# A four-layer graph network on one core: each distance product gets a bank of its own, and the transposed state, the messages and the distances become one block on TensorE

## The chip, the cores and the metric

The kernel runs on one core of a Trainium2 chip. The core has five engines with a queue each: TensorE (PE in the profile, with PEld for its weight loads), VectorE (DVE), ScalarE (ACT), GpSimd (POOL) and SyncE (SP), which only issues transfers here. They take their own instructions in order and wait for one another by semaphores. TensorE writes its products into PSUM, which has eight banks of 128 partitions by 512 fp32 values; this kernel uses all eight. The metric is the device time in microseconds (us) of one execution; lower is better.

## What is computed

Sixteen graphs of 512 nodes with 128 features go through four layers, each with a residual and a layer norm. Cut to what matters, for one graph:

```
# layer 0: gated message passing
h     = conv17(relu(bn(conv1(x))));  x_conv = relu(bn(h) + x)
s     = x @ w_se.T + b_se
A     = exp(-|s_i - s_j|^2)                      # distance products, then exp
msg   = relu(x @ w_msg.T + b_msg)                # messages
x_nmp = (A * adj) @ msg
r, z  = sigmoid(gates of [x_conv, x_nmp], x);  n = tanh(gi_n + r * gh_n)
x1    = layernorm(x + (1 - z) * n + z * x)       # "state" Y, transposed, then normed
# layer 1: attention
X, q, k = leaky(x1 @ W_lin + b), leaky(x1 @ W_q), leaky(x1 @ W_k)
A     = adj * sigmoid(q k^T / sqrt(128)); attended = D^-1/2 A D^-1/2 X
x2    = layernorm(x1 + attended)                 # residual Z1
# layer 2: tangent space
support = adj @ (artanh(|x2|)/|x2| * x2);  x3 = layernorm(x2 + project(expmap0(support)))
# layer 3: degree-normed aggregation, linear, relu
out   = layernorm(x3 + relu(D^-1/2 (adj + I) D^-1/2 x3 W + b))
```

## The kernel before

The graphs go through a software pipeline written out by hand. In **slot** t the front stage (layer 0) of graph t, the middle stage (layer 1) of graph t-1 and the rear stage (layers 2 and 3) of graph t-2 run side by side. Slots 0 to 3 are written out, slots 4 to 14 are a loop, and `ending` writes out slot 15 and the drain of the last two graphs. On each engine a function `body` lists the pieces of a slot in a fixed order; every piece waits for semaphores named after what is ready. The counts `n["f"]`, `n["m"]`, `n["r"]` (and `f_prev`, `m_prev`, `r_prev`) are the graphs that a stage has finished when the piece of this slot (or of the last one) is done. The chunks c = 0 to 3 are blocks of 128 nodes.

The eight banks are CONV (convolution), F0 and F1 (messages, keys, gates), C0 and C1 (distances, attention logits, gates), K0, K1, K2 (many short uses). The profile leaves numbers out of names, so K0, K1 and K2 are all `K` there.

The seam of the slot is where the gates of graph t-1 end and its state goes on to layer 1, while the front stage of graph t begins. Before the change it runs as follows.

- DVE at the end of a slot: `reset`, `rest_of_h1`, `new_input` (L1054, needs the last gate product), `stacked` (L721 and L723, the two factors STL and STR of the distances, from K0 and from ACT's ZR at L433), `kept_state` (L770, XT from the update gate WG), `gated` (L762, L765: the state Y).
- ACT: the update gate WG (L532), ZL and ZR, the tanh (L448), a load of the activation table (L539), four exps of the distances (L453), the copy `keep_x` (L472), four degree sums (L486), the copy X1T of the transposed normed state (L480), the relu of the messages, the copies of queries and keys, the second norm X2 (L414), a logarithm, another table load (L553), the copy XRAW of the linear rows (L506), and four sigmoids of the attention logits (L458).
- PE: distances 0 and 1 into C0 and C1 (L1297), the four transposes of Y into K0 (`state_by_nodes`, L1319), distances 2 and 3 into C0 and C1 again after the exps of 0 and 1, the messages into F0 (L1225), eight taps of the convolution, the four transposes of X1 (L1219), some taps, query, key and linear rows (`projections`; L1351, L1353, L1225), taps, the attention logits (L1364; product c+2 goes into the bank of c after its sigmoid), the support of layer 2 (L1232), the taps of the sum (into K0), and so on. The last aggregation of the rear stage is at L1400.
- DVE at the head of a slot: statistics of the transposed state (`first_norm_stats`, L668), the residual Z1 of layer 1 with its four statistics in between (`first_residual`, L991 and L996), the normed state X1 (`first_norm`, L692), the moments of the second norm, `message_sum` (L829), the sum of H1, the small terms of artanh, `leaky` (L835, L838), `leaky_linear` (L843, needs XRAW), `degree_guard` and `tangent` (the factor and FX at L817, which the support needs), `attention01` (L751: sigmoid times adjacency), `masked0` (L824), `attention23`, `own_loops`, `conv_part` (L944, needs the taps of the sum), `ball_factor`, `second_residual` and its moments, `scaled_norm` (FS at L926, needed by L1400).
- POOL raises variances to the power -0.5 (L336).

Of the kernel before, what the change touches and what calls it, by code (L numbers as in the profile page):

```python
# [68 lines left out]
def adj_resnorm_kernel(nc, xT_d, adjT_d, adj_d, mask_d, weights_d, less_d, rows_d, params_d, sqmat_d, ident_d, out_d):  # L69
    ctx = ExitStack()  # L70
    with ctx:
# [86 lines left out]

        CONV, F0, F1, C0, C1, K0, K1, K2 = (bank(n) for n in ("CONV", "F0", "F1", "C0", "C1", "K0", "K1", "K2"))
        CB = (C0, C1)  # L160

        ev = {n: sem("s_" + n) for n in EVENTS + LN_EVENTS + DMA_EVENTS}
        s_const, s_leading, s_split, s_prep = (sem(n) for n in ("s_const", "s_leading", "s_split", "s_prep"))
# [237 lines left out]
        def _(act):  # L401
# [48 lines left out]
            def exps(n, a, b):  # L450
                for c in range(a, b):
                    act.wait_ge(ev["dist_done"], nth(c, n["f"]))
                    A(A0[:, c, :], CB[c % 2][:, :], ACT.Exp).then_inc(ev["exp_ready"], 1)  # L453

            def sigmoids(n, a, b):
                for c in range(a, b):
# [176 lines left out]
        def _(dve):  # L633
# [150 lines left out]

            def first_norm_stats(n):
                dve.wait_ge(ev["yt_done"], n["m"])
                norm_stats(0, lambda c: cols(K0, c), n["m"])

            def artanh_series(n):
                V.reciprocal(T[:, 8, :], T[:, 2, :])  # L790
# [35 lines left out]

            def message_sum(n):
                dve.wait_ge(ev["msg_done"], n["f"])
                V.tensor_tensor(MSG[:, :, :], chunked(F0), ROWS[:, :].unsqueeze(1).to_broadcast([P, C, P]),  # L829
                                ALU.add).then_inc(ev["msg_sum"], 1)  # L830

            def leaky(n):
# [153 lines left out]
            def first_residual(n, count, previous):  # L986
                dve.wait_ge(ev["x2_ready"], every(previous))

                def residual(c):
                    dve.wait_ge(ev["agg1_done"], nth(finished(n, c), count))  # L990
                    V.scalar_tensor_tensor(Z1[:, c, :], cols(attended_bank(n, c), c), DINV[:, c:c + 1], first_norm_of(n)[:, c, :],  # L991
                                           ALU.mult, ALU.add).then_inc(ev["z1_ready"], 1)

                def stats(c):
                    dve.wait_ge(ev["z1_ready"], nth(c, count))
                    return V.bn_stats(ST[:, 1, c, :], Z1[:, c, :])  # L996

                residual(0)
                residual(1)
                stats(0)  # L1000
                residual(2)
                stats(1)
                residual(3)
                stats(2)
                stats(3).then_inc(ev["ln1_stats"], 1)

            def second_norm_moments(count):
                norm_moments(1, count)
# [1 line left out]
                                       ALU.add).then_inc(ev["var_ready"], 1)  # L1010

            def first_norm(n):
                norm_apply(0, lambda c: cols(K0, c), first_norm_of(n), n["m"], ev["x1_ready"])

            def output(n):
                dve.wait_ge(ev["out_stored"], 16 * (B - 1))
# [39 lines left out]
            def body(t, mid, rear):  # L1056
# [6 lines left out]
                if mid:  # L1063
                    first_norm(n)
                if rear:
                    second_norm_moments(n["r"])
                message_sum(n)
                if not n["first"]:
# [4 lines left out]
                    artanh_series(n)  # L1073
                if mid:
                    leaky(n)
                    leaky_linear(n)
                if rear:
                    degree_guard(n)
                    tangent(n)
                if mid:  # L1080
                    attention01(n)
                masked0(n)
# [22 lines left out]
                reset(n)  # L1105
                if following:
                    rest_of_h1(n["f_next"], n["f"])
                new_input(n)
                if following:
                    stacked(n["f_next"])  # L1110
                    kept_state(n["f"])
                    gated(n["f"])

            def ending():
                a, b, c = counts(dve, B - 1), counts(dve, B), counts(dve, B + 1)
                first_norm_stats(a)
                first_residual(a, a["r"], a["r_prev"])
                first_norm(a)
                second_norm_moments(a["r"])
                message_sum(a)  # L1120
                sum_of_h1(a["f"], a["f_prev"])
# [1 line left out]
                artanh_ratio(a)  # L1123
                artanh_series(a)
                leaky(a)
                leaky_linear(a)
                degree_guard(a)
                tangent(a)
                attention01(a)
                masked0(a)  # L1130
                attention23(a)
# [17 lines left out]
                first_norm_stats(b)  # L1149
                first_norm(b)  # L1150
                first_residual(a, a["m"], a["m_prev"])
                second_norm_moments(a["m"])
                leaky(b)
                leaky_linear(b)
# [9 lines left out]
                scaled_attention(b)  # L1164
                ball_factor(b)
                first_residual(b, b["m"], b["m_prev"])
                second_norm_moments(b["m"])
                second_residual(b)
                tangent_norm(c)
# [22 lines left out]
        def _(pe):  # L1192
# [85 lines left out]
            def sum_taps(n):  # L1278

                pe.wait_ge(ev["hsl_ready"], n["f"])  # L1280
                pe.wait_ge(ev["str_ready"], n["f"])
                pe.wait_ge(ev["x_raw"], n["m"])
                if n["first"]:
                    pe.wait_ge(s_split, 4)
                taps(S_SUM, 0, ODD, K0[:, 0:PH], HSH[:, :], HSL[:, :], ODD).then_inc(ev["conv2_sum"], 1)
# [7 lines left out]
                                  stop=(last and k == 3 * len(terms)))  # L1293
                return done

            def distances(c):
                mm(CB[c % 2][:, :], cols(STL, c), STR[:, :], start=True, stop=True).then_inc(  # L1297
                    ev["dist_done"], 1)

            def first_taps(n):  # L1300
                pe.wait_ge(ev["h1_ready"], n["f"])
# [2 lines left out]
                    pe.wait_ge(s_split, 2)  # L1304
                even_taps(0, 8)

            def distances01(n):
                pe.wait_ge(ev["str_ready"], n["f"])
                pe.wait_ge(ev["w_ready"], n["f_prev"])
                distances(0)  # L1310
                pe.wait_ge(ev["gate_u"], n["f_prev"])
                distances(1)

            def state_by_nodes(n):
                pe.wait_ge(ev["y_ready"], n["m"])
                pe.wait_ge(ev["d_kept"], n["m_prev"])
                pe.wait_ge(ev["str_ready"], n["f"])
                for c in range(C):
                    last = nc.tensor.transpose(cols(K0, c), cols(Y, c), IDENT[:, :])  # L1319
                last.then_inc(ev["yt_done"], 1)  # L1320

            def distances23(n):
                pe.wait_ge(ev["exp_ready"], nth(0, n["f"]))
                distances(2)
                pe.wait_ge(ev["exp_ready"], nth(1, n["f"]))
                distances(3)

            def messages(n):
                pe.wait_ge(ev["gate_t"], n["f_prev"])
                pe.wait_ge(ev["x_loaded"], 16 * n["f"])  # L1330
                if n["first"]:
                    pe.wait_ge(s_plain_w, 48)
                    pe.wait_ge(s_less, 1)
                rows_of(F0, X_IN, plain(F_MSG)).then_inc(ev["msg_done"], 1)

            def first_norm_by_features(n):
                if not n["drain"]:
# [3 lines left out]
            def support(n):  # L1341
                pe.wait_ge(ev["xt_ready"], n["r"])
                if not n["drain"]:
                    pe.wait_ge(ev["adjr_loaded"], 16 * n["r"])
                if not n["last"]:
                    pe.wait_ge(ev["res_scaled"], n["r_prev"])
                aggregate_nodes(lambda c: support_bank(n, c), adjacency(n), FX, ev["agg2_done"])

            def projections(n):
                pe.wait_ge(ev["x1t_ready"], n["m"])  # L1350
                mm(query_bank(n)[:, :], plain(F_Q), X1T[:, :], start=True, stop=True).then_inc(ev["q_done"], 1)  # L1351
                pe.wait_ge(ev["msg_sum"], n["f"])
                mm(F0[:, :], plain(F_K), X1T[:, :], start=True, stop=True).then_inc(ev["k_done"], 1)  # L1353
                rows_of(K0, X1T, plain(F_LIN)).then_inc(ev["x_done"], 1)

            def attention(n):
                pe.wait_ge(ev["q_ready"], n["m"])
                pe.wait_ge(ev["k_ready"], n["m"])
                for c in range(C):
                    if c < 2:  # L1360
                        pe.wait_ge(ev["exp_ready"], nth(c + 2, n["f"]))
# [118 lines left out]

            def ending():
                a, b, c = counts(pe, B - 1), counts(pe, B), counts(pe, B + 1)
                distances01(a)
                state_by_nodes(a)
                distances23(a)
                messages(a)
                first_taps(a)
                first_norm_by_features(a)
                even_taps(8, EVEN)
# [99 lines left out]
```

## Time and profile before

| | |
|---|---|
| median of 3 runs | 797.41 us (796.39 to 798.12) |
| the profiled execution | 798.0 us, its span 796.2 us |
| mean granted clock of TensorE | 0.964 of full speed |
| busy, PE / DVE / ACT / POOL | 715.7 (90%) / 625.2 (79%) / 424.7 (53%) / 135.3 us (17%) |
| one slot of the loop | 45.3 us (from one `new_input` to the next) |

The span runs from the first to the last instruction of the profiled execution. A busy share is a mean over the whole span; a matmul counts as busy while it is in the pipeline, so a PE that is busy nine tenths of the time can still have waits that matter. The time of an engine's wait stands in brackets behind the instruction that ended it, with the instruction that released it.

### The profile page before, as it was taken

The page shows a single profiled execution, that of the slowest core. Times are in us where ns is not written, and L with a number is a line of the kernel's source. Part 1 is how long each engine was busy: PE and PEld are TensorE (multiplying, and loading weights), DVE is VectorE, ACT ScalarE, POOL GpSimd, SP SyncE. Part 2 cuts the span into 40 slices and gives each one's busy share as a digit, 9 for nine tenths or more (in the row PEclk, how much of TensorE's full clock was granted, in tenths as well). Part 3 has the DMA queues.
Part 4 walks back from the last instruction along what each step waited for, and adds up shares of the span by engine and source line. Part 5 has one row for each costly group of instructions (what it writes and reads, how often), then busy time and mean ns, then how long its engine had stood idle before and what let it go on. Part 6 is the DMA issues. An engine that isn't in the chain of part 4 may idle for free.

```text
span 796.2 us, 12758 instructions
## 1 busy us (share of the span) xinstructions
PE 715.7 (90%) x3984; PEld 542.6 (68%) x3984; DVE 625.2 (79%) x2080; ACT 424.7 (53%) x881; POOL 135.3 (17%) x151
## 2 busy tenths in 40 slices
PE   3889999999999999999999999999999999998653
PEld 1766777777676877767776777767677776765531
DVE  7456788888878887888888888887888888876655
ACT  4164737556473755657373755647374655624431
POOL 0000111211122111211121121121121121111221
PEclk8889999999999999999999999999999999999776
DMA  5303241150605133060514224060423215101000
GB/s 198 119 14 129 97 158 68 57 169 14 224 14 171 66 108 116 23 215 13 193 44 162 75 66 158 13 224 13 171 66 122 102 45 192 54 14 54 0 14 27
DMA packets 46586, 75.33 MB, mean 95 GB/s; under 512 B 4065, under 2 KB 12769, under 8 KB 46433
## 3 DMA queue, kind: packets, MB, share of 16 engines
q1 hardware_dynamic: 46560, 75.02, 27.6%
q8 instruction: 12, 0.20, 0.1%
q14 instruction: 14, 0.11, 0.0%
HBM read 70.82 MB, written 4.19 MB: 94 GB/s over the span
## 4 chain that ended last, share of the span: by engine, by line
DVE 40%; PE 36%; issue 11%; ACT 9%; POOL 3%; DVEq 1%; DMA 0%; SPq 0%; ACTq 0%; POOLq 0%
PE K L1400 7%; DVE BIG L751 5%; PE C L1292 4%; PE CONV L1266 4%; DVE A L824 4%; PE F L1292 3%; ACT X L414 2%; DVE X L692 2%; POOL RSTD L336 2%; DVE Z L866 2%; ACT L553 2%; PE F L1353 2%; DVE FS L926 2%; DVE Z L991 2%; DVE ST L668 2%
## 5 line engine op out<-in xcount | busy, mean ns | idle before, releaser
L336 POOL TENSOR_TENSOR RSTD<-VEPS,POW 128x4 f32<-128x4 f32 x48 | 48.8, 1017 | 341.6 <-DVE VEPS L686 341.6
L1266 PE MATMUL CONV<-H1H,WH 128*128 128x256 f32 x288 | 85.6, 297 | 0.0
L1266 PE MATMUL CONV<-H1L,WH 128*128 128x256 f32 x288 | 81.4, 283 | 0.0
L1266 PE MATMUL CONV<-H1H,WL 128*128 128x256 f32 x288 | 81.2, 282 | 0.0
L1400 PE MATMUL K<-ADJR,FS 128*128 128x512 f32 x112 | 52.9, 617 | 10.1 <-DVE FS L926 10.1
L1364 PE MATMUL C<-QT,KT 128*128 128x512 f32 x128 | 61.6, 606 | 0.1
L1232 PEld LDWEIGHTS K<-XS,BIG 128*128 128x128 f32 x496 | 57.8, 192 | 1.3
L1232 PE MATMUL K<-XS,BIG 128*128 128x128 f32 x496 | 57.9, 275 | 0.0
L1232 PEld LDWEIGHTS K<-FX,ADJR 128*128 128x128 f32 x448 | 51.1, 192 | 9.9 <-issue 8.2
L1372 PE MATMUL F<-A,MSG 128*128 128x512 f32 x128 | 57.5, 592 | 0.0
L1266 PEld LDWEIGHTS CONV<-H1L,WH 128*128 128x128 f32 x288 | 55.2, 192 | 0.0
L1266 PEld LDWEIGHTS CONV<-H1H,WH 128*128 128x128 f32 x288 | 55.2, 192 | 0.0
L1266 PEld LDWEIGHTS CONV<-H1H,WL 128*128 128x128 f32 x288 | 55.1, 191 | 0.0
L1232 PE MATMUL K<-FX,ADJR 128*128 128x128 f32 x448 | 53.4, 277 | 0.0
L523 ACT ACTIVATE XCH<-XC,BI 128x512 fp32r<-128x512 f32 x16 | 11.5, 722 | 68.2 <-DVE XC L950 68.2
L453 ACT ACTIVATE A<-C 128x512 f32<-128x512 f32 x64 | 34.8, 595 | 23.1 <-PE C L1297 23.1
L458 ACT ACTIVATE BIG<-C 128x512 f32<-128x512 f32 x64 | 38.0, 596 | 15.4 <-PE C L1364 14.1
L1400 PEld LDWEIGHTS K<-ADJR,FS 128*128 128x128 f32 x112 | 20.8, 196 | 36.4 <-issue 36.4
L500 ACT ACTIVATE JUNK<-K 128x128 bf16<-128x128 f32 x60 | 15.8, 277 | 50.4 <-PE K L1232 50.4
L1364 PEld LDWEIGHTS C<-QT,KT 128*128 128x128 f32 x128 | 21.6, 188 | 28.6 <-ACT BIG L458 19.5
L751 DVE TENSOR_TENSOR BIG<-BIG,ADJM 128x512 f32<-128x512 f32 x60 | 39.9, 685 | 1.4 <-ACT BIG L458 1.4
L824 DVE TENSOR_TENSOR A<-A,ADJF 128x512 f32<-128x512 f32 x64 | 39.8, 685 | 0.0
(251 smaller groups left out, 1932.1 us busy)
## 6 DMA issues: line engine op xcount, KB each, us to landing
ADJF<-in_adjT SPq DMA_DIRECT2D x16, 1024.0 KB, 5.3
ADJN<-in_adj SPq DMA_DIRECT2D x16, 1024.0 KB, 7.7
ADJM<-in_adjT SPq DMA_DIRECT2D x15, 1024.0 KB, 6.9
ADJR<-in_adjT SPq DMA_DIRECT2D x14, 1024.0 KB, 5.2
X_IN<-in_xT SPq DMA_DIRECT2D x16, 256.0 KB, 2.6
out<-OUT SPq DMA_DIRECT2D x16, 256.0 KB, 3.2
BIG<-in_weights SPq DMA_DIRECT2D x1, 1088.0 KB, 5.4
BIG<-in_weights SPq DMA_DIRECT2D x1, 576.0 KB, 8.7
```

What stands on the lines that cost most here:

```text
L336: nc.gpsimd.tensor_tensor(RSTD[:, row, :], VEPS[:, row, :], POW[:, 0, :], ALU.pow).then_inc(ev[f"ln{layer}_rstd"], 1)
L414: A(dst[:, c, :], src(c), ACT.Identity, bias=SHIFT[:, layer, c:c + 1], scale=RSTD[:, row, c:c + 1]).then_inc(done, 1)
L453: A(A0[:, c, :], CB[c % 2][:, :], ACT.Exp).then_inc(ev["exp_ready"], 1)
L458: A(SIG[:, c, :], CB[c % 2][:, :], ACT.Sigmoid, scale=float(P) ** -0.5).then_inc(ev["sig_ready"], 1)
L751: last = V.tensor_tensor(A1[:, c, :], SIG[:, c, :], attention_adjacency(n)[:, c, :], ALU.mult)
L824: last = V.tensor_tensor(A0[:, c, :], A0[:, c, :], ADJF[:, c, :], ALU.mult)
L1232: last = mm(cols(out(c), c), adj[:, k, c * P:(c + 1) * P], rows[:, k, :], start=(k == 0), stop=(k == C - 1))
L1266: last = mm(out, w[:, at_col + k * P:at_col + (k + 1) * P], h[:, k:k + PH], start=(k == 0 and i == 0), stop=(k == count - 1 and i == 2))
L1292: done = mm(bank[:, :], wgt[i], mov[j], start=(first and k == 1), stop=(last and k == 3 * len(terms)))
L1364: mm(CB[c % 2][:, :], cols(KT, c), QT[:, :], start=True, stop=True).then_inc(ev["att_done"], 1)
L1372: last = mm(F1[:, :], MSG[:, c, :], A0[:, c, :], start=(c == 0), stop=(c == C - 1))
L1400: last = mm(last_sums_bank(n)[:, :], FS[:, k, :], adjacency(n)[:, k, :], start=(k == 0), stop=(k == C - 1))
```

## The change

- **Banks.** The four distance products get a bank each, `DB = (C0, C1, F1, K1)`, and the exps read from there. No distance waits for an exp any more. Attention logits still use C0 and C1.
- **PE order.** The transposes of Y, the messages and the four distances are one block in this order. The transposes go into F0 and the messages into K0 (they were the other way round). The key product and the support get new waits.
- **DVE order.** `kept_state` moves ahead of `new_input`. The four statistics of the residual move out of `first_residual` into `first_residual_stats`, behind `first_norm`. `leaky_linear` moves behind `degree_guard` and `tangent`.

The order of ACT, POOL and SP is left as it is. The diff, cut to its core:

```diff
+        DB = (C0, C1, F1, K1)
...
-                    A(A0[:, c, :], CB[c % 2][:, :], ACT.Exp).then_inc(ev["exp_ready"], 1)
+                    A(A0[:, c, :], DB[c][:, :], ACT.Exp).then_inc(ev["exp_ready"], 1)
...
             def first_norm_stats(n):
                 dve.wait_ge(ev["yt_done"], n["m"])
-                norm_stats(0, lambda c: cols(K0, c), n["m"])
+                norm_stats(0, lambda c: cols(F0, c), n["m"])
...
-                V.tensor_tensor(MSG[:, :, :], chunked(F0), ROWS[:, :]...
+                V.tensor_tensor(MSG[:, :, :], chunked(K0), ROWS[:, :]...
...
-                def stats(c):
+                for c in range(C):
+                    residual(c)
+
+            def first_residual_stats(count):
+                for c in range(C):
                     dve.wait_ge(ev["z1_ready"], nth(c, count))
-                    return V.bn_stats(ST[:, 1, c, :], Z1[:, c, :])
-
-                residual(0)
-                residual(1)
-                stats(0)
...
+                    last = V.bn_stats(ST[:, 1, c, :], Z1[:, c, :])
+                last.then_inc(ev["ln1_stats"], 1)
...
             def first_norm(n):
-                norm_apply(0, lambda c: cols(K0, c), first_norm_of(n), n["m"], ev["x1_ready"])
+                if not n["drain"]:
+                    dve.wait_ge(ev["z1_ready"], every(n["m_prev"]))
+                norm_apply(0, lambda c: cols(F0, c), first_norm_of(n), n["m"], ev["x1_ready"])
...
                 if mid:
                     first_norm(n)
                 if rear:
+                    first_residual_stats(n["r"])
                     second_norm_moments(n["r"])
...
                 if mid:
                     leaky(n)
-                    leaky_linear(n)
                 if rear:
                     degree_guard(n)
                     tangent(n)
+                if mid:
+                    leaky_linear(n)
...
                     rest_of_h1(n["f_next"], n["f"])
+                if following:
+                    kept_state(n["f"])
                 new_input(n)
                 if following:
                     stacked(n["f_next"])
-                    kept_state(n["f"])
                     gated(n["f"])
...
             def sum_taps(n):
                 pe.wait_ge(ev["hsl_ready"], n["f"])
+                pe.wait_ge(ev["msg_sum"], n["f"])
...
-            def distances(c):
-                mm(CB[c % 2][:, :], cols(STL, c), STR[:, :], start=True, stop=True).then_inc(
-                    ev["dist_done"], 1)
+            def distances(n):
+                pe.wait_ge(ev["str_ready"], n["f"])
+                pe.wait_ge(ev["w_ready"], n["f_prev"])
+                pe.wait_ge(ev["gate_u"], n["f_prev"])
+                pe.wait_ge(ev["r_ready"], n["f_prev"])
+                pe.wait_ge(ev["res_scaled"], n["r_prev"])
+                for c in range(C):
+                    mm(DB[c][:, :], cols(STL, c), STR[:, :], start=True, stop=True).then_inc(ev["dist_done"], 1)
...
             def state_by_nodes(n):
                 pe.wait_ge(ev["y_ready"], n["m"])
-                pe.wait_ge(ev["d_kept"], n["m_prev"])
-                pe.wait_ge(ev["str_ready"], n["f"])
+                pe.wait_ge(ev["gate_t"], n["m"])
                 for c in range(C):
-                    last = nc.tensor.transpose(cols(K0, c), cols(Y, c), IDENT[:, :])
+                    last = nc.tensor.transpose(cols(F0, c), cols(Y, c), IDENT[:, :])
                 last.then_inc(ev["yt_done"], 1)
+            def messages(n):
+                pe.wait_ge(ev["str_ready"], n["f"])
                 pe.wait_ge(ev["x_loaded"], 16 * n["f"])
...
-                rows_of(F0, X_IN, plain(F_MSG)).then_inc(ev["msg_done"], 1)
+                rows_of(K0, X_IN, plain(F_MSG)).then_inc(ev["msg_done"], 1)
...
             def support(n):
...
+                pe.wait_ge(ev["exp_ready"], every(n["f"]))
                 aggregate_nodes(lambda c: support_bank(n, c), adjacency(n), FX, ev["agg2_done"])
...
             def projections(n):
...
+                pe.wait_ge(ev["x1_ready"], every(n["m"]))
+                mm(F0[:, :], plain(F_K), X1T[:, :], start=True, stop=True).then_inc(ev["k_done"], 1)
                 pe.wait_ge(ev["msg_sum"], n["f"])
-                mm(F0[:, :], plain(F_K), X1T[:, :], start=True, stop=True).then_inc(ev["k_done"], 1)
                 rows_of(K0, X1T, plain(F_LIN)).then_inc(ev["x_done"], 1)
...
-                distances01(n)
                 if mid:
                     state_by_nodes(n)
-                distances23(n)
-                messages(n)
+                    messages(n)
+                distances(n)
+                if not mid:
+                    messages(n)
                 first_taps(n)
```

The ending has the same moves for slot 15; in the drain only the split of the residual's statistics is new.

## Rows read from the trace of the kernel before

**Rows 1.** Windows: us, busy time per engine (instructions), granted clock, DMA share, GB/s; ten slots of the loop.

```profile
221.21:674.25 453.04, 434.37 (x2492) 331.59 (x2491) 379.08 (x1271) 262.29 (x552) 83.57 (x90) 1.00 0.31 104
```

**Rows 2.** The chain that ended last, in one slot: start, us on the chain, what.

```profile
357.10 0.78 ACT ZR L433
...
359.32 0.60 DVE XT L770
...
374.25 0.61 ACT XRAW L506
```

**Rows 3.** Timeline of DVE, same slot: start, us, line, tiles, count, [idle before, releaser].

```profile
357.12 0.69 DVE L1054 TENSOR_TENSOR GT<-GT,C 128x512 f32<-128x512 f32 x1 [0.45 <-PE C L1292]
...
360.55 0.69 DVE L765 TENSOR_TENSOR Y<-NG,XT 128x512 f32<-128x512 f32 x1
362.15 0.89 DVE L668 BATCH_NORM_STATS2 ST<-K 128x6 f32<-128x128 f32 x4 [0.91 <-PE K L1319]
...
363.99 0.61 DVE L991 SCALAR_TENSOR_TENSOR Z<-K,DINV,X 128x128 f32<-128x128 f32 x2
...
365.82 1.35 DVE L692 TENSOR_SCALAR X<-K,NMEAN,RSTD 128x128 f32<-128x128 f32 x4
...
374.88 0.69 DVE L843 SCALAR_TENSOR_TENSOR XX<-XRAW 128x512 f32<-128x512 f32 x1 [2.06 <-ACT XRAW L506]
...
376.37 0.69 DVE L817 TENSOR_TENSOR FX<-X,T 128x512 f32<-128x512 f32 x1
376.98 1.28 DVE L751 TENSOR_TENSOR BIG<-BIG,ADJM 128x512 f32<-128x512 f32 x2
...
384.57 0.75 DVE L944 SCALAR_TENSOR_TENSOR XC<-K,SC,XT 128x512 f32<-128x512 f32 x1
```

**Rows 4.** Timeline of PE, same slot.

```profile
361.48 0.63 PE L1319 MATMUL K<-IDENT,Y 128*128 128x128 f32 x4 [0.36 <-DVE Y L765]
361.87 0.71 PE L1297 MATMUL C<-STR,STL 128*128 128x512 f32 x2
362.41 1.05 PE L1225 MATMUL F<-WF,X_IN 128*128 128x128 f32 x8
363.22 0.36 PE L1266 MATMUL CONV<-H1H,WH 128*128 128x256 f32 x1
...
367.22 0.66 PE L1219 MATMUL K<-IDENT,X 128*128 128x128 f32 x4 [0.90 <-DVE X L692]
...
368.79 1.02 PE L1351 MATMUL K<-X1T,WF 128*128 128x512 f32 x2
...
373.52 3.85 PE L1364 MATMUL C<-QT,KT 128*128 128x512 f32 x8
377.32 0.93 PE L1232 MATMUL K<-FX,ADJR 128*128 128x128 f32 x6
...
383.73 0.28 PE L1266 MATMUL K<-HSH,WL 128*128 128x256 f32 x1
...
391.37 3.67 PE L1400 MATMUL K<-ADJR,FS 128*128 128x512 f32 x8 [0.58 <-DVE FS L926]
```

**Rows 5.** Timeline of ACT, same slot.

```profile
355.56 0.69 ACT L532 ACTIVATE WG<-C,NBZ 128x512 f32<-128x512 f32 x1
...
360.92 1.09 ACT L453 ACTIVATE A<-C 128x512 f32<-128x512 f32 x2 [1.06 <-PE C L1297]
362.38 1.09 ACT L453 ACTIVATE A<-C 128x512 f32<-128x512 f32 x2 [0.38 <-PE C L1297]
...
366.24 0.19 ACT L486 ACTIVATION_READ_ACCUMULATOR JUNKD<-ADJN 128x1 f32 x1
367.91 0.60 ACT L480 ACTIVATE X1T<-K 127x512 f32<-127x512 f32 x1 [1.48 <-PE K L1219]
...
374.74 1.29 ACT L458 ACTIVATE BIG<-C 128x512 f32<-128x512 f32 x2
```

**Rows 6.** Timeline of POOL, same slot: the first norm's power.

```profile
364.02 1.01 POOL L336 TENSOR_TENSOR RSTD<-VEPS,POW 128x4 f32<-128x4 f32 x1 [7.28 <-DVE VEPS L686]
```

More of the change, by code:

```diff
@@ L828, in message_sum @@
                 dve.wait_ge(ev["msg_done"], n["f"])
-                V.tensor_tensor(MSG[:, :, :], chunked(F0), ROWS[:, :].unsqueeze(1).to_broadcast([P, C, P]),
+                V.tensor_tensor(MSG[:, :, :], chunked(K0), ROWS[:, :].unsqueeze(1).to_broadcast([P, C, P]),
                                 ALU.add).then_inc(ev["msg_sum"], 1)
@@ L992, in residual @@
                                            ALU.mult, ALU.add).then_inc(ev["z1_ready"], 1)
-                def stats(c):
+                for c in range(C):
+                    residual(c)
+            def first_residual_stats(count):
+                for c in range(C):
                     dve.wait_ge(ev["z1_ready"], nth(c, count))
-                    return V.bn_stats(ST[:, 1, c, :], Z1[:, c, :])
-                residual(0)
-                residual(1)
-                stats(0)
[L1001 to L1005, printed above, removed]
+                    last = V.bn_stats(ST[:, 1, c, :], Z1[:, c, :])
+                last.then_inc(ev["ln1_stats"], 1)
             def second_norm_moments(count):
@@ L1118, in ending @@
                 first_norm(a)
+                first_residual_stats(a["r"])
                 second_norm_moments(a["r"])
@@ L1125, in ending @@
                 leaky(a)
-                leaky_linear(a)
                 degree_guard(a)
                 tangent(a)
+                leaky_linear(a)
                 attention01(a)
@@ L1151, in ending @@
                 first_residual(a, a["m"], a["m_prev"])
+                first_residual_stats(a["m"])
                 second_norm_moments(a["m"])
@@ L1166, in ending @@
                 first_residual(b, b["m"], b["m_prev"])
+                first_residual_stats(b["m"])
                 second_norm_moments(b["m"])
@@ L1305, in first_taps @@
                 even_taps(0, 8)
-            def distances01(n):
-                pe.wait_ge(ev["str_ready"], n["f"])
[L1309 to L1312, printed above, removed]
             def state_by_nodes(n):
                 pe.wait_ge(ev["y_ready"], n["m"])
-                pe.wait_ge(ev["d_kept"], n["m_prev"])
-                pe.wait_ge(ev["str_ready"], n["f"])
-                for c in range(C):
-                    last = nc.tensor.transpose(cols(K0, c), cols(Y, c), IDENT[:, :])
[L1320 to L1329, printed above, removed]
+                pe.wait_ge(ev["gate_t"], n["m"])
+                for c in range(C):
+                    last = nc.tensor.transpose(cols(F0, c), cols(Y, c), IDENT[:, :])
+                last.then_inc(ev["yt_done"], 1)
+            def messages(n):
+                pe.wait_ge(ev["str_ready"], n["f"])
                 pe.wait_ge(ev["x_loaded"], 16 * n["f"])
@@ L1360, in attention @@
                     if c < 2:
-                        pe.wait_ge(ev["exp_ready"], nth(c + 2, n["f"]))
+                        pe.wait_ge(ev["exp_ready"], nth(c, n["f"]))
                     else:
@@ L1482, in ending @@
                 a, b, c = counts(pe, B - 1), counts(pe, B), counts(pe, B + 1)
-                distances01(a)
                 state_by_nodes(a)
-                distances23(a)
                 messages(a)
+                distances(a)
                 first_taps(a)
```

## The prediction

> **What bounds the kernel.** I read the busy time by windows first, to see that the loop repeats: ten slots take 453.04 us, 45.3 each, at a granted clock of 1.00 [rows 1]. PE is busy 434.37 us of that, 43.4 a slot, so if its work stays, a slot can lose 1.9 us at most. The gain has to come out of waits, so the second view is the chain of waits through one slot (here 357 to 402 us). It changes engine many times, and in the seam it passes through every piece that the change touches: ACT's ZR, DVE's two factors, `kept_state`, the two halves of Y, the transposes, the statistics, the residual and its statistics, X1, the query product, the second norm, the table load, XRAW, and then DVE without a break [rows 2]. The third view is the timeline of each engine in that slot, for the waits in brackets: DVE waits 0.45 us before `new_input`, 0.91 before the statistics, 2.06 before `leaky_linear` [rows 3]; PE 0.36 before the transposes of Y, 0.90 before those of X1, 0.58 before the last aggregation [rows 4]; ACT 1.48 before X1T [rows 5]. The reader should see that no engine is the bound all through: the slot is one loop of hand-overs, and an edit pays where its hand-over ends last.
>
> **The change step by step**, in the times of that slot; a minus is earlier than before.
>
> *`kept_state` ahead of `new_input`.* It holds 0.60 us of the chain, between the second factor and Y [rows 2]. In its new place DVE is idle for 0.45 us, up to 357.12 [rows 3], and its input WG is there at 356.25 (355.56 + 0.69) [rows 5]. It takes about 0.6, so `new_input` comes 0.1 to 0.2 later and ends at 357.9 to 358.0. STL waits for ZR until 357.88 anyway [rows 2], so I cost the delay at nothing: the idle time and ZR hide it. If that cover were gone it would cost up to 0.60, the whole of this step. Y ends at 360.64 and not at 361.24: **-0.60**.
>
> *The block on PE.* The transposes came 0.24 after Y's end (361.48 against 361.24) [rows 3, 4], so now 360.88. They hold PE for 0.39 (361.48 to 361.87), the messages for 0.81 (362.41 to 363.22), two distances for 0.54 (361.87 to 362.41) [rows 4]. Messages start at 361.27, distances at 362.08, the first tap at 363.16 against 363.22: **-0.06**. Behind the transposes' wait for Y now stand the messages and all four distances; before, two distances ran ahead of it. That shifts the exps: the third distance went at 361.87 and its exp at 362.38, 0.51 apart [rows 4, 5], so the first exp is at 362.59 and not at 360.92. The waits that the distances gain (WG, gates, last residual) all end before 358. Transposes into F0, messages into K0 are the same instructions, and the key product still comes after X1 is written; I cost the banks at nothing.
>
> *Statistics behind X1.* They start at 361.55 (362.15 - 0.60) [rows 3]. The residual starts at 363.39; two take 0.61 with a step of 0.28, so four end at 364.56. POOL's power, before 364.02 to 365.03, ends at 364.43 [rows 6] and no longer waits for anybody. So X1 starts at 364.6 instead of 365.82: 0.6 from Y and 0.6 from the statistics; it ends at 365.95: **-1.2**. PE was idle for 0.90 before 367.22, so its taps were done at 366.32 [rows 4], now at 366.26. That is the later of the two: the transposes of X1 go at 366.26, **-0.96**. The second norm's moments come after X1's 1.26 and four statistics of 0.89 in all, about 0.3 earlier than before, early enough for `message_sum` and X2.
>
> *ACT takes part of this back.* Four exps in a row: a pair takes 1.09, of which one is 0.60, so the step is 0.49 [rows 5]. From 362.59 the last ends at 364.66 instead of 363.47 (362.38 + 1.09): +1.19. Behind them on ACT's queue stand `keep_x`, four degree sums and X1T. The last sum ended at 366.43, now at 367.62; X1T can start there or, with the overlap of neighbours, 0.1 sooner, against 367.91 [rows 5]. Bounds -0.29 and -0.38; I take 367.56, **-0.35**. ACT's wait of 1.48 is used up, and PE waits for X1T now: its query was 1.57 after the transposes (368.79 - 367.22) [rows 4], so it would be ready at 367.83.
>
> That step is a measured one; the Trainium skill (ScalarE: Activation LUTs, "What ACT_TABLE_LOAD costs") gives an ACTIVATE with immediates 186 ns plus 0.833 ns a column and an overlap of 93 ns between neighbours, by which I estimate 0.52 us a step here. By it the exps would end 0.1 later, and the sum below would be some 1.3 us smaller in all; the pair of 1.09 us decides for 0.49.
>
> *Query to sigmoid.* X1T ends at 368.16; the query followed X1T's end by 0.28 before (368.79 against 368.51) [rows 4, 5], and was perhaps held by the taps. Ends: 368.30 to 368.44; I take 368.39, **-0.4**. From here ACT is a queue without holes (keys, X2, logarithm, table load, XRAW), so XRAW and the sigmoids come 0.4 earlier. The third logits product waits for the first sigmoid, so the support moves by 0.4 with it. FX ended at 377.06, and the support went at 377.32 while the logits ended at 377.37 (373.52 + 3.85) [rows 3, 4]: FX may have held it by nothing or by up to 0.2; with FX some 3 us earlier (next step) that goes. I take 0.1: support **-0.5**, and so the taps of the sum.
>
> *`leaky_linear` behind `tangent`.* Guard, factor and FX took from 375.57 to 377.06 on DVE after XX; before XX DVE waited 2.06 [rows 3]. The 1.5 us now fits into the wait. XX comes at 374.48, `attention01` 0.6 later at 375.1 instead of 376.98: -1.9. The second sigmoid ended at 376.03 (374.74 + 1.29) [rows 5], now at 375.63, in time for the second chunk. DVE then runs ahead by 1.9 until `conv_part`, which needs the last tap of the sum: 384.01 before (383.73 + 0.28) [rows 4], now 383.51. `conv_part` goes at 383.55 instead of 384.57 [rows 3]: **-1.0**, the rest (0.9) is a new wait there. Bounds: -0.56 if the support did not move, -1.9 if the taps were early enough.
>
> *To the end of the slot.* From `conv_part` DVE, POOL and DVE lead to FS without slack, and the last aggregation waited 0.58 for FS while PE itself comes 0.5 earlier: it can follow by 1.08 [rows 4]. So it starts **-1.0**, and the gates and the next seam with it. The slot becomes 44.3 us, above PE's 43.4.
>
> **The sum.** Slots 2 to 15 have all three stages: 14 x 1.0 = 14.0 us. Slot 1 has no rear stage, so neither residual nor `tangent`; I put it at zero. In the drain the residual and its statistics are pulled apart without an X1 to be gained: together 1.83 (363.99 to 365.82), apart 1.17 + 0.89 [rows 3], 0.23 each for two graphs: +0.5. Net -13.5. The profiled execution (798.0, the span and 1.8 around it) goes to 784.5; the median lies 0.6 below it, so 783.9, rounded to **784.0**.
>
> **Rivals.**
> - *No room for `kept_state`.* Y stays at 361.24, the first exp is at 363.19, X1T at 368.16, the query 0.15 later than before. X1 still gains 0.6, and the tangent's step still brings `conv_part` to the last tap, now at 384.06: -0.5. 14 x 0.5 - 0.5 gives 791. For: 0.45 of idle time is less than 0.60. Against: ZR covers the rest. Chance 0.10.
> - *ACT eats the seam.* X1T stays at 367.91; support gains only the 0.1, `conv_part` 0.65: 14 x 0.65 - 0.5 gives 789. For: only 0.3 us of slack is left. Chance 0.15.
> - *ACT does not hold X1T.* The query comes with the transposes, -0.96; support -1.06, last aggregation -1.6: 14 x 1.6 gives 775. Against: ACT's rows add up to 367.5. Chance 0.05.
> - *ACT makes it slower.* Each us by which X1T passes 367.91 pushes query, sigmoids and support by one. The gains further on are worth 0.28 + 0.65 at most, so from 368.8 on, a first exp at 363.8 or later, the kernel loses; at 364.2 it is 0.4 a slot, 803. It needs the distances 1.2 us later than PE's rows give, by a wait among their new five that I have wrong. Chance 0.12: 0.05 that it comes out within 0.2%, 0.07 slower.
>
> **Numbers.** My forecast has 0.58, with its own range 779 to 787 (1.3 to 0.8 us a slot, from the bounds of X1T, query and FX). The range 779 to 791 takes in both smaller gains. Faster by over 0.2% (about what a measurement of this kernel can tell from no change): 0.58 + 0.10 + 0.15 + 0.05 = 0.88; within it 0.05; slower 0.07.
>
> **What would show it.** Slots of 44.3 us; no idle before `new_input`; exps in one run of four; X1T released by ACT's own queue and not by PE; a PE wait of about 0.5 us before the query in place of the 0.90 before X1's transposes; no wait at `leaky_linear` to speak of, and a new one of about 0.9 at `conv_part` for the taps of the sum; a shorter wait before the last aggregation. I am wrong if X1T starts later than before, if `conv_part` does not wait for PE, or if the last aggregation does not move with it.

## The result and the profile after

The changed kernel takes **778.65 us** (median of 4 runs, 776.58 to 779.28) against 797.76 of the kernel before (four runs, among them the three of its table), a ratio of 0.9753 (95% interval 0.9723 to 0.9783). The profiled execution took 778.3 us, its span 776.5. The change gains 19 us where 13.5 were forecast; the time is 0.35 us below the range.

The chain that ended last, by engine, and the windows over the loop's ten slots in the kernel after:

```profile
PE 80%; ACT 10%; DVE 5%; issue 3%; POOL 1%; DMA 0%; SPq 0%; ACTq 0%; POOLq 0%; DVEq 0%
```

```profile
218.34:658.10 439.76, 433.33 (x2493) 334.30 (x2492) 382.56 (x1271) 260.19 (x552) 83.83 (x90) 1.00 0.32 107
```

The chain was DVE 40% and PE 36%; now it is PE's. A slot takes 43.98 us instead of 45.30 (453.04 / 10, [rows 1]), and PE is busy for 43.33 of them. By that reading 0.65 us is left to lose, but PE's busy time is no floor, and neither were the 43.4 from which the prediction took its "1.9 us at most": the kernel of experiment 9 has slots of 43.19, 2.11 less than before, with PE busy for 43.08 of them. Part of what counts as busy goes with the waits: the query's two products count 1.12 us here, behind a wait, and 1.02 before the change, without one.

The same seam in the kernel after, between the `new_input` at 350.27 and the next at 394.26. Lines have moved: L1310 distances, L1323 transposes of Y, L1224 of X1, L1350 query, L1237 support, L1271 taps, L992 residual, L693 X1, L1001 its statistics, L454 exps, L487 degree sums, L481 X1T, L844 `leaky_linear`, L752 `attention01`, L945 `conv_part`. PE first, from the third product of the last gate:

```profile
349.78 0.39 PE L1298 MATMUL C<-XCH,WL 128*128 128x512 f32 x1
...
353.78 0.66 PE L1323 MATMUL F<-IDENT,Y 128*128 128x128 f32 x4
354.27 1.06 PE L1230 MATMUL K<-WF,X_IN 128*128 128x128 f32 x8
355.08 0.71 PE L1310 MATMUL C<-STR,STL 128*128 128x512 f32 x2
...
358.95 0.60 PE L1224 MATMUL K<-IDENT,X 128*128 128x128 f32 x4
361.15 1.12 PE L1350 MATMUL K<-X1T,WF 128*128 128x512 f32 x2 [0.54 <-ACT X1T L481]
...
365.98 3.86 PE L1364 MATMUL C<-QT,KT 128*128 128x512 f32 x8
369.68 3.73 PE L1237 MATMUL K<-FX,ADJR 128*128 128x128 f32 x32
...
376.00 0.28 PE L1271 MATMUL K<-HSH,WL 128*128 128x256 f32 x1
...
383.14 3.67 PE L1400 MATMUL K<-ADJR,FS 128*128 128x512 f32 x8
```

DVE and ACT in the same slot:

```profile
350.27 0.68 DVE L1053 TENSOR_TENSOR GT<-GT,C 128x512 f32<-128x512 f32 x1
...
353.03 0.69 DVE L766 TENSOR_TENSOR Y<-NG,XT 128x512 f32<-128x512 f32 x1
354.47 0.89 DVE L669 BATCH_NORM_STATS2 ST<-F 128x6 f32<-128x128 f32 x4 [0.75 <-PE F L1323]
...
356.31 1.13 DVE L992 SCALAR_TENSOR_TENSOR Z<-K,DINV,X 128x128 f32<-128x128 f32 x4
357.47 1.37 DVE L693 TENSOR_SCALAR X<-F,NMEAN,RSTD 128x128 f32<-128x128 f32 x4
...
367.35 0.69 DVE L844 SCALAR_TENSOR_TENSOR XX<-XRAW 128x512 f32<-128x512 f32 x1 [0.36 <-ACT XRAW L507]
367.95 1.29 DVE L752 TENSOR_TENSOR BIG<-BIG,ADJM 128x512 f32<-128x512 f32 x2
...
376.32 0.75 DVE L945 SCALAR_TENSOR_TENSOR XC<-K,SC,XT 128x512 f32<-128x512 f32 x1 [0.68 <-PE K L1271]
```

```profile
355.59 1.09 ACT L454 ACTIVATE A<-C 128x512 f32<-128x512 f32 x2 [2.59 <-PE C L1310]
356.56 0.61 ACT L454 ACTIVATE A<-F 128x512 f32<-128x512 f32 x1
...
360.40 0.21 ACT L487 ACTIVATION_READ_ACCUMULATOR JUNKD<-ADJN 128x1 f32 x1
360.50 0.60 ACT L481 ACTIVATE X1T<-K 127x512 f32<-127x512 f32 x1
361.22 0.63 ACT L477 ACTIVATE MSG<-MSG 128x512 f32<-128x512 f32 x1
```

The slot is shorter than the 44.3 us that were named; every other sign is there: no idle time before `new_input`, four exps in a run, X1T straight behind ACT's own degree sums with no wait, PE's 0.90 before X1's transposes gone and a wait of 0.54 before the query, only 0.36 left at `leaky_linear`, a new wait of 0.68 at `conv_part` for the taps of the sum, and the 0.58 before the last aggregation gone (a shorter one was forecast). To compare places, I count from the start of that third gate product, 356.69 before (0.39 ahead of the 357.08 at which `new_input` was released) and 349.78 after:

| | before | after | moved | forecast |
|---|---|---|---|---|
| Y starts | 3.86 | 3.25 | -0.61 | -0.60 |
| transposes of Y | 4.79 | 4.00 | -0.79 | -0.60 |
| first tap | 6.53 | 6.31 | -0.22 | -0.06 |
| transposes of X1 | 10.53 | 9.17 | -1.36 | -0.96 |
| X1T | 11.22 | 10.72 | -0.50 | -0.35 |
| query | 12.10 | 11.37 | **-0.73** | -0.4 |
| support | 20.63 | 19.90 | -0.73 | -0.5 |
| last tap of the sum | 27.04 | 26.22 | -0.82 | -0.5 |
| `conv_part` | 27.88 | 26.54 | -1.34 | -1.0 |
| last aggregation | 34.68 | 33.36 | -1.32 | -1.0 |

### The profile page after: what moved, and what is told of

It is laid out like the page before. It is cut to its first block, busy times and chain, and to the rows that moved or that the text cites. A ratio compares the mean times of both kernels' runs of the same rounds, so it can differ in the third digit from the quotient of the medians.

```text
span 776.5 us, 12808 instructions
## 1 busy us (share of the span) xinstructions
PE 712.1 (92%) x3984; PEld 545.3 (70%) x3984; DVE 629.8 (81%) x2080; ACT 421.5 (54%) x881; POOL 135.1 (17%) x151
## 4 chain that ended last, share of the span: by engine, by line
PE 80%; ACT 10%; DVE 5%; issue 3%; POOL 1%; DMA 0%; SPq 0%; ACTq 0%; POOLq 0%; DVEq 0%
PE K L1237 14%; PE K L1400 7%; PE C L1364 7%; PE C L1298 7%; PE F L1372 7%; PE CONV L1271 6%; PE K L1271 6%; PE F L1298 5%; ACT JUNKD L487 4%; PE K L1230 4%; ACT A L454 3%; PE K L1350 2%; PE K L1258 2%; PE F L1352 2%; PE CONV L1205 2%
## 5 line engine op out<-in xcount | busy, mean ns | idle before, releaser
L1271 PE MATMUL CONV<-H1H,WH 128*128 128x256 f32 x288 | 84.3, 293 | 0.0
L1271 PE MATMUL CONV<-H1L,WH 128*128 128x256 f32 x288 | 81.5, 283 | 0.0
L1271 PE MATMUL CONV<-H1H,WL 128*128 128x256 f32 x288 | 81.2, 282 | 0.0
L1237 PEld LDWEIGHTS K<-XS,BIG 128*128 128x128 f32 x496 | 57.8, 192 | 1.3
L1237 PE MATMUL K<-XS,BIG 128*128 128x128 f32 x496 | 57.9, 275 | 0.0
L1237 PEld LDWEIGHTS K<-FX,ADJR 128*128 128x128 f32 x448 | 52.2, 192 | 6.7 <-issue 6.7
L1271 PEld LDWEIGHTS CONV<-H1H,WH 128*128 128x128 f32 x288 | 55.3, 192 | 0.7
L1271 PEld LDWEIGHTS CONV<-H1L,WH 128*128 128x128 f32 x288 | 55.2, 192 | 0.7
L1271 PEld LDWEIGHTS CONV<-H1H,WL 128*128 128x128 f32 x288 | 55.0, 191 | 0.0
L1237 PE MATMUL K<-FX,ADJR 128*128 128x128 f32 x448 | 52.3, 275 | 0.0
L347 POOL TENSOR_TENSOR T<-T,POW 128x4 f32<-128x4 f32 x16 | 19.3, 1205 | 129.2 <-ACT JUNK L501 129.2
L752 DVE TENSOR_TENSOR BIG<-BIG,ADJM 128x512 f32<-128x512 f32 x60 | 39.9, 685 | 1.4 <-ACT BIG L459 1.4
L454 ACT ACTIVATE A<-C 128x512 f32<-128x512 f32 x32 | 17.4, 595 | 41.7 <-PE C L1310 41.7
```

The costliest lines, as they stand in the source:

```text
L454: A(A0[:, c, :], DB[c][:, :], ACT.Exp).then_inc(ev["exp_ready"], 1)
L752: last = V.tensor_tensor(A1[:, c, :], SIG[:, c, :], attention_adjacency(n)[:, c, :], ALU.mult)
L1237: last = mm(cols(out(c), c), adj[:, k, c * P:(c + 1) * P], rows[:, k, :], start=(k == 0), stop=(k == C - 1))
L1271: last = mm(out, w[:, at_col + k * P:at_col + (k + 1) * P], h[:, k:k + PH], start=(k == 0 and i == 0), stop=(k == count - 1 and i == 2))
```

## The experiments

The theory after the result: the slot is a loop of hand-overs, Y to exps to ACT's queue to X1T to query on one side, and DVE's order from `tangent` to `conv_part` on the other. Its rivals give the gain to the banks and the block, or to X1's lead. A slot's length is the mean of the loop's slots, from one `new_input` to the next; the ratio is to the kernel before on the same chip.

**1. `kept_state` back.**

```diff
-                if following:
-                    kept_state(n["f"])
                 new_input(n)
                 if following:
                     stacked(n["f_next"])
+                    kept_state(n["f"])
                     gated(n["f"])
```

> The changed kernel with kept_state put back between the factors and the state. Theory, the hand-over loop: in the changed kernel Y ends 0.61 us earlier after the last gate product than before, ACT's exps start from it and hold X1T, and X1T releases the query. So the loss is Y's 0.61 plus whatever the transposes wait longer when PE stands idle (0 to 0.2): the query 0.6 to 0.8 later, slots of 44.6 to 44.8 instead of 43.98, and over 14 slots 787 to 790. PE is idle before the transposes of Y again. Rival, that the gain comes from the two other moves on DVE and PE hides the rest: no change, 778 to 780.

788.92 us, ratio 0.9872 (0.985 to 0.9894), slots of 44.57: +0.59 on the changed kernel. As the theory says. In its timeline of PE, the transposes wait for Y with PE idle:

```profile
404.18 0.66 PE L1322 MATMUL F<-IDENT,Y 128*128 128x128 f32 x4 [0.64 <-DVE Y L766]
```

Y ended at 404.12, so the hand-over takes 0.06 even so, and not the 0.24 of the kernel before.

**2. The statistics back** in between the residual, ahead of X1.

```diff
-                for c in range(C):
-                    residual(c)
...
+                residual(0)
+                residual(1)
+                stats(0)
...
+                stats(3).then_inc(ev["ln1_stats"], 1)
```

> The changed kernel with the residual's statistics interleaved again, ahead of X1. Theory, ACT holds X1T: X1 comes 0.6 later and the transposes of X1 end at about 10.4 us after the last gate product instead of 9.8, which is still before ACT is through with its degree sums (10.7), so X1T and the query stay where they are: slots 43.9 to 44.2, and DVE saves 0.2 a slot on statistics; 777 to 781. Rival, that X1's lead of 1.4 us is on the path: query 0.5 later, slots of 44.5, 786.

778.59 us, ratio 0.9744 (0.9723 to 0.9765), slots of 44.00: nothing lost. PE waits for X1 again, and then does not wait for X1T. Its timelines of PE and ACT:

```profile
403.09 0.66 PE L1224 MATMUL K<-IDENT,X 128*128 128x128 f32 x4 [0.43 <-DVE X L693]
404.71 1.12 PE L1350 MATMUL K<-X1T,WF 128*128 128x512 f32 x2
```

```profile
404.05 0.60 ACT L481 ACTIVATE X1T<-K 127x512 f32<-127x512 f32 x1
```

The third gate product is at 393.33 here, so X1's transposes come at 9.76, 0.59 later than after, but X1T at 10.72 and the query at 11.38, where they were. The whole lead that the statistics gave X1 is idle time at the query.

**3. `leaky_linear` back** ahead of the guard and the tangent.

```diff
                     leaky(n)
+                    leaky_linear(n)
                 if rear:
                     degree_guard(n)
                     tangent(n)
-                if mid:
-                    leaky_linear(n)
```

> The changed kernel with leaky_linear ahead of degree_guard and tangent again. Theory: DVE gets 1.5 us behind from there to conv_part, where it has 0.68 of wait to lose; so conv_part is no longer released by PE and comes 0.8 later, FS and the last aggregation too: slots of 44.7 to 44.8, 789 to 791, and a wait of PE before the last aggregation of 0.7 to 0.9. The support moves by 0.1 to 0.2 for FX. Rival, that the gain is all in the seam and this move only shifts a wait: slots of 44.1, 780.

790.25 us, ratio 0.9893 (0.987 to 0.9915), slots of 44.72: +0.74. `conv_part` no longer waits, DVE waits 1.96 at `leaky_linear`, and PE 0.63 before the last aggregation, much as before the change (2.06 and 0.58, [rows 3, 4]).

**4. The block alone**: the three edits of 1, 2 and 3 together, so that only the banks and PE's order differ from the kernel before.

> The changed kernel with all three moves on DVE undone: only the banks and PE's block are left. Theory: the block shifts the exps behind Y and PE gains nothing from it: query 0.6 later than in the changed kernel, DVE 2.1 later at attention01 less 0.68 of wait at conv_part, so the last aggregation 1.4 later: slots of 45.3 to 45.4, 796 to 799, no gain over the kernel before. Rival, that the banks and the block carry a part of their own, since no distance waits for an exp: slots of 44.6, 788.

798.91 us, ratio 1.0001 (0.9988 to 1.0015), slots of 45.32 against 45.30. The block by itself, in this order, is worth nothing, and the parts add up: 0.59 + 0.02 + 0.74 = 1.35 against 1.34 lost here.

**5. DVE's moves alone**: PE's order and banks of the kernel before, with the three moves (the reverse of 1, 2 and 3 in it).

> The kernel before with the three moves on DVE alone: PE's order and the banks are the old ones. Theory, the gain comes from DVE's moves and the block only costs ACT time: Y is as early as in the changed kernel, two distances go ahead of it, so ACT's exps begin 1.6 us earlier and ACT no longer holds X1T; the transposes of Y wait for the distances by 0.2 to 0.4, X1's transposes come 0.2 later, and the query is bound by PE's taps, 0.3 to 0.4 earlier than in the changed kernel: slots of 43.5 to 43.8, 772 to 776. Rival, the block is needed to make use of the early Y: slots of 44.3 to 44.6, 783 to 787.

774.19 us, ratio 0.9692 (0.9676 to 0.9708), slots of 43.80. Faster than the changed kernel by 0.18 a slot: in the order that it has there, the block costs (experiment 7 turns that round). The timeline of PE, and of ACT's X1T:

```profile
350.57 0.71 PE L1301 MATMUL C<-STR,STL 128*128 128x512 f32 x2
351.12 0.60 PE L1323 MATMUL K<-IDENT,Y 128*128 128x128 f32 x4
351.73 0.99 PE L1301 MATMUL C<-STR,STL 128*128 128x512 f32 x2
...
357.79 1.02 PE L1355 MATMUL K<-X1T,WF 128*128 128x512 f32 x2
...
362.94 3.79 PE L1368 MATMUL C<-QT,KT 128*128 128x512 f32 x8 [0.26 <-DVE KT L838]
```

```profile
356.93 0.60 ACT L480 ACTIVATE X1T<-K 127x512 f32<-127x512 f32 x1 [0.60 <-PE K L1223]
```

With two distances ahead of Y, ACT has its sums done in time and waits 0.60 for the transposes; the query comes without a wait, 10.94 after the third gate product (346.85), 0.43 earlier than in the changed kernel.

**6. Degree sums later on ACT**, behind the sigmoids; `degree_guard` behind `own_loops` on DVE, and POOL's degree power behind its norm power.

```diff
                 keep_x(n)
-                if rear:
-                    degrees(n)
...
                     sigmoids(n, 0, C)
                 if rear:
+                    degrees(n)
                     support_norms(n)
```

> The changed kernel with ACT's four degree sums (2.5 us) moved behind the sigmoids, where ACT waits 3.0 us for the support; degree_guard moves behind own_loops on DVE, and POOL raises the degrees after the norms (slots 0 to 14). Theory, ACT holds X1T: X1T goes right after the transposes, 0.85 earlier, and the query as soon as PE has done its taps; PE's wait of 0.54 before the query goes, and PE becomes the bound: slots of 43.4 to 43.5, 770 to 773. Rival, the query is held by something else (X1, PE): slots of 43.9 to 44.0, 778.

774.2 us, ratio 0.9696 (0.9678 to 0.9714), slots of 43.60. PE's wait before the query is gone, so it was ACT that held it. I had the slots 0.1 to 0.2 too short: PE now waits 0.27 for KT before the logits.

**7. Distances ahead of the messages** in the block.

```diff
                 if mid:
                     state_by_nodes(n)
-                    messages(n)
                 distances(n)
-                if not mid:
-                    messages(n)
+                messages(n)
```

> The changed kernel with the distances ahead of the messages in the block. Theory, ACT holds X1T and its queue starts with the first distance: exps 0.8 earlier, X1T 0.8 earlier, query when PE is ready, PE's wait of 0.54 gone: slots of 43.4 to 43.5, 770 to 773, the same as with the degree sums moved. Rival, the order inside the block is indifferent: 778.

772.12 us, ratio 0.9667 (0.9646 to 0.9687), slots of 43.60. The exps start 0.8 earlier and the same wait goes; the same 0.28 for KT is what comes next, which I had not foreseen here either. The timeline of PE:

```profile
357.64 1.02 PE L1350 MATMUL K<-X1T,WF 128*128 128x512 f32 x2
...
362.81 3.79 PE L1364 MATMUL C<-QT,KT 128*128 128x512 f32 x8 [0.28 <-DVE KT L839]
```

**8. The late wait last**, in the kernel before.

```diff
+                pe.wait_ge(ev["d_kept"], n["m_prev"])
+                pe.wait_ge(ev["str_ready"], n["f"])
                 pe.wait_ge(ev["y_ready"], n["m"])
-                pe.wait_ge(ev["d_kept"], n["m_prev"])
-                pe.wait_ge(ev["str_ready"], n["f"])
```

> The kernel before with one edit: in state_by_nodes the wait for Y stands behind the two waits that have long been met, not ahead of them. The transposes came 0.24 after Y's end in the kernel before and 0.06 in the changed one, also where PE stood idle. Theory, the waits written behind the late one are worked off after it: transposes 0.06 to 0.1 after Y, 0.15 to 0.18 a slot, 795 to 796. Rival, the 0.24 belongs to PE's idle state or to the bank: no change, 797 to 798.

797.99 us, ratio 0.9997 (0.9982 to 1.0012): no change that the time can tell, and not the 795 to 796 that were expected. In its timelines Y ended at 362.31 and the transposes started at 362.46, 0.15 apart instead of 0.24, and the loop's slots take 45.20 instead of 45.30. So, read from one execution of each, the order of the waits is worth 0.09, which is half of the hand-over's shrinking from 0.24 to 0.06. What the other half is, no run separates: the changed kernel's list has two waits instead of three, with Y's still ahead, and its transposes go into another bank.

**9. Distances first, and the keys early**: the kernel of 7, with `leaky` ahead of `artanh_series` on DVE.

```diff
                     artanh_ratio(n)
-                    artanh_series(n)
                 if mid:
                     leaky(n)
                 if rear:
+                    artanh_series(n)
                     degree_guard(n)
```

> The kernel with the distances ahead of the messages, and on DVE leaky (queries and keys) ahead of artanh_series. In that kernel PE waits 0.28 us a slot for KT before the attention logits, and nowhere else that the trace names; the series takes 0.8 us of DVE ahead of KT, and its result is needed only by tangent. Theory, the slot is now a loop through KT and PE is full behind it: the wait goes, slots of 43.3 to 43.4, 767 to 769. Rival, something else stands at once behind the wait for KT: slots of 43.5 to 43.6, 771 to 773.

**766.94 us**, ratio 0.9603 (0.9579 to 0.9627), slots of 43.19, 0.1 shorter than expected: the wait for KT is gone and no other took its place before the logits. This is the fastest of all, 12 us under the changed kernel. In its windows, over nine of the loop's slots, PE counts as busy all the time but for 1.0 us:

```profile
250.00:640.00 390.00, 389.00 (x2247) 301.28 (x2246) 344.56 (x1146) 233.80 (x497) 78.05 (x81) 1.00 0.33 109
```

**10. DVE's moves and the keys early**: the kernel of 5 with the edit of 9.

> The kernel with the three moves on DVE and PE's old order and banks, and leaky ahead of artanh_series. Theory: its wait of 0.26 for KT goes, slots of 43.5 to 43.6, 770 to 772; what is left against the kernel with the distances first (0.2 a slot) are the waits between the distances and the exps, the only thing that a bank for each distance takes away. Rival, the banks save nothing: the same time as the kernel with the distances first and the keys early.

769.85 us, ratio 0.9637 (0.9612 to 0.9662), slots of 43.45. The 0.26 that are left to kernel 9 are what the banks and the block in the order of 7 are worth together. They lie in the seam on PE, as its timelines here and in kernel 9 show:

```profile
344.80 3.73 PE L1236 MATMUL K<-XS,BIG 128*128 128x128 f32 x32
...
349.45 0.99 PE L1301 MATMUL C<-STR,STL 128*128 128x512 f32 x2
350.27 1.05 PE L1229 MATMUL F<-WF,X_IN 128*128 128x128 f32 x8
```

```profile
344.18 3.73 PE L1237 MATMUL K<-XS,BIG 128*128 128x128 f32 x32
347.95 0.66 PE L1323 MATMUL F<-IDENT,Y 128*128 128x128 f32 x4
...
349.38 1.05 PE L1230 MATMUL K<-WF,X_IN 128*128 128x128 f32 x8
```

From the products of XS to the messages it is 5.47 us here and 5.20 there. With two banks the second pair of distances holds PE for 0.82 (349.45 to 350.27, its wait for two exps), with four a pair takes 0.55 (355.08 to 355.63 in the kernel after). But the seams differ in more: behind XS the first distance follows after 3.48 us here, and the transposes, which come first in kernel 9, after 3.77, because they need Y; PE counts as busy meanwhile. What the banks are worth with the old order, no run separates.

## Why the prediction was wrong

The direction, the path and every wait that went or came were right; the sum was 30% short of the measured gain, and the range ended 0.35 us too high. The step that failed is **"Query to sigmoid"**, with the X1T that it takes over from "ACT takes part of this back": X1T at -0.35 and the query at -0.4. They measured -0.50 and -0.73. Of these 0.33, 0.18 is the hand-over from X1T to the query and 0.15 X1T itself. Everything behind the query moved much as worked out from it, so the 0.33 went through to the end of the slot: 1.32 and not 1.0. Over the slots up to 14 that is 3.9 us, which would have left the time at 780.1, inside the range. What took it out, as far as the profiled executions tell, is slot 15, whose clock had no term in the sum: 1.5 of the 1.9 us by which that slot gained more than forecast.

- *`kept_state`*: -0.61 against -0.60, and ZR and the idle time did hide it. Experiment 1 gives 0.59 a slot.
- *The block on PE*: I took the 0.24 between Y's end and the transposes as fixed. It is 0.06 with the new list of waits (and 0.15 in experiment 8); of these 0.18 the transposes take 0.10 back, for they hold PE for 0.49 (353.78 to 354.27) and not for 0.39. So the distances were 0.1 earlier than forecast, and the exps with them: first exp at 5.81 instead of 5.90. This is 0.1 of the 0.15 by which X1T was off; the rest is the overlap behind the last degree sum, 0.11, of which I had taken half.
- *X1*: -1.36 for the transposes, against -0.96. Of these 0.40, 0.16 is the earlier start of the taps (-0.22, not -0.06) and 0.08 their pace (2.86 from the first tap to the transposes, 2.94 before). For 0.16 I ended PE's taps at the end of the last product in the pipeline (366.32) instead of at its step (366.04 + 0.12); in the kernel after, the transposes start 0.11 behind the start of the last tap (358.84 to 358.95). It made no difference, because ACT held X1T, as forecast. Experiment 2 shows it: 0.6 us of X1 given back, and the time stays.
- *Query behind X1T*: I took 0.14 to 0.28 for this hand-over and measured 0.05 (361.10 to 361.15; it is 0.05 or 0.06 in experiments 1, 2 and 3 too). In the kernel before the 0.28 belonged to PE's taps [rows 4, 5], of which the last started one step of 0.12 ahead of the query at 368.79; I wrote "perhaps held by the taps" and still carried most of it over. The timeline of PE in the kernel before:

```profile
368.67 0.28 PE L1266 MATMUL CONV<-H1H,WL 128*128 128x256 f32 x1
```

- *Support*: -0.73. The logits moved by -0.63 only, because the query's two products take 0.96 behind PE's wait and took 0.86 before. From the logits to the support it is 3.70 instead of 3.80, and 3.80 again in experiment 3, where FX is late: this is the 0.1 for FX, as forecast. The support's products then took 0.1 less up to the taps of the sum (3.49 instead of 3.59), so these moved by -0.82.
- *`leaky_linear`*: right. DVE reached `attention01` 2.1 earlier (-1.9 forecast) and lost the surplus at `conv_part`, where it waited 0.68. Experiment 3 prices it at 0.74.
- *Slots 2 to 15*: slot 15 went from 44.47 to 41.59, by 2.9 and not 1.0. PE's wait before its last aggregation fell from 1.83 to 0.88 there, and its granted clock stayed up; the timeline of PE in the kernel before and in the kernel after, and the windows of the kernel before:

```profile
708.50 5.21 PE L1400 MATMUL K<-ADJR,FS 128*128 128x512 f32 x8 [1.83 <-DVE FS L926]
```

```profile
691.02 3.67 PE L1400 MATMUL K<-ADJR,FS 128*128 128x512 f32 x8 [0.88 <-DVE FS L927]
```

```profile
709.00:711.00 2.00, 2.00 (x3) 0.67 (x2) 1.35 (x6) 0.85 (x2) 0.54 (x1) 0.50 0.00 0
```

Behind the longer wait the eight products took 1.5 us more; in the windows from 709 to 711 the clock of the kernel before is 0.50, the lower level of 1.2 GHz, and after the change it is 1.00 from 690 to 699. I had no term for this. That the shorter wait is what kept the clock up is likely, but not shown (see the last section), and these are single executions.

- *Slot 1 and the drain*: the start of slot 1 came 0.5 later, slot 1 took 0.2 more, and the drain 76.8 us instead of 77.5, where I had +0.5. Among the other runs here the start ends at 46.7 to 48.6, slot 1 takes 36.5 to 39.3 and the drain 76.3 to 78.9, so these are not readings of the change.

In sum: the loop's step was short by 0.3 in each of 13 slots (3.9 us, with the slots before the loop's steady state counted in), slot 15 by 1.9, the drain by 1.2, less 0.8 at the start; 6.2 us together, the gap between the forecast 784.5 of the profiled execution and its 778.3.

Of the rivals, "ACT does not hold X1T" was the nearest in time, and it is the wrong mechanism for this kernel: ACT did hold X1T, at 10.72. Experiments 6 and 7 are that rival made true, and they gain a further 0.38 a slot. Its 775 rested on 1.6 a slot; 6 and 7 have 1.7 (45.30 to 43.60).

The four exps after start at steps of 0.48 to 0.49 (355.59, two of them to 356.56; the third and fourth at 356.56 and 357.04), as the pair in the trace of the kernel before had it. The Trainium skill (ScalarE: Activation LUTs, "What ACT_TABLE_LOAD costs") had led me to an estimate of 0.52 us for the step between neighbouring ACTIVATEs of 512 columns; the trace's pair was the better source, and 0.1 us at X1T hung on it.

## What to carry to other kernels

A wait that is measured between two engines is no constant of theirs: before carrying it into a forecast, ask whether the waiting engine was still busy (then the gap is its own work) and which waits stand in its list, and in which order. Where an edit takes a stall away, look for the queue that the freed result meets next: here half of the seam's lead (X1) was lost at once at ACT's queue, and a swap of two pieces on PE, with no instruction more or less, brought 0.4 us a slot of it back. A bank for every product can be worth only the waits that it takes away: with the block in its better order it came to 0.26 us a slot here once KT no longer held the loop, and to nothing, or less, while the reordering that came with it fed another queue late.

## What the runs showed of the hardware

- The hand-over from DVE's Y to PE's transposes took 0.24 us with three waits and the late one first, 0.15 with the late one last, and 0.06 with another list of two, again the late one first, and into another bank, the last with PE idle for 0.64 as well as with PE busy. Number, order and bank are not separated.
- PE's granted clock fell to 0.50 around a wait of 1.83 us before the last aggregation of slot 15 (eight products in 5.21 and, in experiment 8, 5.37 instead of 3.67): in the kernel before at 708.2, in the last 0.3 us of the wait, in experiment 8 about 1 us behind its end. With waits of 1.59 it fell once (experiment 3, 5.18) and once not (experiment 4, 3.67); with 0.88 and 0.89 it did not in any of the eight other kernels.
